# Cross-attention with a gated residual on one core: the last stage reordered, and its residual added by VectorE from a loaded x

## The chip, the cores and the metric

The kernel runs on one core of a Trainium2 chip. The metric is the device time of one execution in microseconds, lower is better. TensorE (PE), VectorE (DVE), ScalarE (ACT), GpSimd (POOL) and SyncE (SP) run their own instruction streams and wait for each other through semaphores; SP issues most of the transfers.

## The reference

x is (4, 1024, 1024), ctx (4, 2048, 512), all float32.

```python
memory_proj = jnp.einsum('bme,de->bmd', memory, W_mem)
scores = jnp.einsum('bnd,bmd->bnm', hidden_states, memory_proj) / jnp.sqrt(jnp.float32(D))
attn = jax.nn.softmax(scores, axis=-1)
memory_context = jnp.einsum('bnm,bmd->bnd', attn, memory_proj)
gate_input = jnp.concatenate([hidden_states, memory_context], axis=-1)
gate = jax.nn.sigmoid(jnp.einsum('bnf,df->bnd', gate_input, W_gate) + b_gate)
fused = hidden_states + gate * memory_context
return _rmsnorm(fused, norm_w)      # fused * rsqrt(mean(fused^2) + 1e-6) * norm_w
```

## The kernel before

The 4096 rows of x are 32 units of 128 rows; two units are a pair, 16 pairs (NPAIR). Each operand of a matmul is split into a rounded part and a remainder (ACT rounds, DVE subtracts), and a product runs three passes.

Four stages follow each other. The first makes q (x times W_mem) and weights for the gate. The second computes, pair by pair, the part of the gate that comes from x ("zx", with the bias), in seven products of 12 matmuls, and stores it. The third is the attention: scores, softmax, exchange of the probabilities through DRAM, and the weighted sum of memory, am, stored for each unit. The **last stage**, about 1270 us to the end, is the one that changes. For each pair it multiplies am (256 rows, 512 columns) by two weight matrices of 512 x 1024: one gives the other part of the gate, one the memory context. Each is done in Strassen's manner with seven products of half size ("gate 1" to "gate 7", "context 1" to "context 7"; `gate_product` and `context_product` on PE), six matmuls of 512 columns each, so a pair is 14 products, 84 matmuls. The tile of a pair has two units u and two halves h of 512 columns; a quadrant is (u, h).

What belongs to a pair p in the last stage:

- DVE: `gate_part` (line 1264) adds a product in PSUM to the loaded zx in place, six times (products 2 to 7). `transpose_am` (line 253), `sums_of_am` (line 1222) and `split_at` (line 305) prepare the operands of the next pair. `context_part` (line 1270) adds a product to a copied one in the output tile `c_u`, twice. `gated` (line 1278) multiplies a context quadrant by its gate into `c_u`, four times; (1, 0) is done at the start of the next pair. `scale` (line 1284) multiplies a unit of `c_u` by the norm factor and the norm weights.
- ACT: `seed_z` (line 856), `gate` (the sigmoid, line 861), `copy_c` (three copies of a product, line 865), `split_at` (line 792), `square` (line 871) with the sum over a row.
- POOL: `add_xres` (line 648), two transfers that add x to `c_u` in SBUF, each after the last gated products of its unit; `inverse_root` (lines 653, 656), the norm factor.
- SP: `load_zx` (line 586), `load_am` (line 582), `store_out` (line 592), in that order in `pair_out`.

Gate tile and `c_u` are double buffered by the parity of the pair. The orders are written out by hand in each engine's program. In a pair's stretch DVE and ACT also square and scale the pair before: `square(p - 1)` and `scale(p - 1)`. PE's first product of a pair waits until all of DVE's six gate parts of the pair before are done (`gz_ev`), and context 1 until its last `gated` is done (`gc_ev`):

```python
def pair_c(p, par, first=False):
    gate_product(p, par, 1)
    context_product(p - 1, 1 - par, 7, first=first)
    gate_product(p, par, 2)
    gate_product(p, par, 3)
    for n in range(1, 5):
        context_product(p, par, n)
        gate_product(p, par, n + 3)
    context_product(p, par, 5)
    context_product(p, par, 6)
```

For the last pair the kernel before already loads x into `c_xlast` and adds it on DVE (`residual`, line 1474).

Of the kernel before, what the change touches and what calls it, by code (L numbers as in the profile page):

```python
# [5 lines left out]
ALU = mybir.AluOpType  # L6
# [14 lines left out]
def build(nc, x, mem, w_mem, w_gate, b_gate, norm_w, out):  # L21
# [28 lines left out]
    with ExitStack() as ctx:  # L50
# [121 lines left out]
        c_xlast = F[:, 28 * KW:36 * KW]  # L172
# [48 lines left out]
        nw_loaded, xlast_loaded = sem("nw_loaded"), sem("xlast_loaded")  # L221
# [4 lines left out]
        xres_added = [sem(f"xres_added{u}") for u in range(2)]  # L226
        fused_done, sq_done, var_done, rstd_done = sem("fused_done"), sem("sq_done"), sem("var_done"), sem("rstd_done")
        out_ready, out_stored = sem("out_ready"), [sem(f"out_stored{r}") for r in range(2)]
# [98 lines left out]
        COPY_B, COPY_22, COPY_12 = range(1, 4)  # L327
# [6 lines left out]
        def _(sp):  # L334
# [255 lines left out]
            def store_out(p, par, u):  # L590
                sp.wait_ge(out_ready, p * 2 + (u + 1))
                sp.dma_start(out_rows[bass.ds(p * (2 * P) + u * P, P), :], unit_tile(c_u[par], u)
                             ).then_inc(out_stored[par], 16)
# [8 lines left out]
            for n in range(NPROD):  # L602
# [7 lines left out]
            sp.dma_start(c_xlast.rearrange("p (u d) -> p u d", u=2),  # L610
                         x_rows[ROWS - 2 * P:ROWS, :].rearrange("(u p) d -> p u d", u=2)).then_inc(xlast_loaded, 16)
# [14 lines left out]
            pair_out(1, 1)  # L626
# [4 lines left out]
            pair_out(NPAIR - 1, 1, ahead=False, am_ahead=False)  # L631
            store_out(NPAIR - 1, 1, 0)
            for n, h in enumerate((1, 0)):
                sp.wait_ge(out_ready, NUNIT + n)
                sp.dma_start(out_rows[ROWS - P:ROWS, BANK * h:BANK * (h + 1)], quad(c_u[1], 1, h)
                             ).then_inc(out_stored[1], 16)
            sp.wait_ge(out_stored[0], 16 * NPAIR)
            sp.wait_ge(out_stored[1], 16 * (NPAIR + 1))

        @block.gpsimd  # L640
        def _(pool):
# [17 lines left out]
            def pair_pool(p, par):  # L659
                for u in range(2):  # L660
                    add_xres(p, par, u)
# [11 lines left out]
        def _(act):  # L673
# [193 lines left out]
            def square(p, par, u, wait=True):  # L867
                act.wait_ge(xres_added[u], p * 16 + 16)
# [6 lines left out]
            def pair_act(p, par, i=None, norm=True, following=True):  # L875
# [3 lines left out]
                if i is not None:  # L879
# [841 lines left out]
```

## Time and profile before

| | us |
|---|---|
| median of 3 runs (lowest, highest) | 1581.92 (1580.89, 1583.91) |
| the profiled execution | 1583.89 |
| its span | 1582.2 |
| PE busy | 1536.3 (97%) |
| DVE busy | 1046.1 (66%) |
| ACT busy | 541.0 (34%) |
| POOL busy | 53.8 (3%) |

The span is from the first to the last instruction of one profiled execution. The PE row counts matmuls, whose records overlap by some 0.16 us. Times in the rows below are microseconds from the start of the span.

### The profile page before, as it was taken

To read this page: it belongs to the slowest core of one execution; us is meant where nothing else is said; L and a number is where in the kernel's file an instruction comes from. 1 tells how busy PE (TensorE), PEld (TensorE's weight loads), DVE (VectorE), ACT (ScalarE), POOL (GpSimd) and SP (SyncE) were. 2 spreads that over 40 slices of the span, in tenths; PEclk is the share of its full clock that TensorE was granted. 3 is DMA by queue.
4 is the path that set the end of the run, shared out by engine and by line. 5 is a ranking of instruction groups with operands and counts; after the bars stand their busy time and mean duration, and the time that the engine had idled before them with its cause. 6 is when DMAs were issued, how large, how long until landed. Compare 5 with 4: busy or idle time off the path is not lost.

```text
span 1582.2 us, 21437 instructions
## 1 busy us (share of the span) xinstructions
PE 1536.3 (97%) x6720; PEld 1262.2 (80%) x6720; DVE 1046.1 (66%) x1474; ACT 541.0 (34%) x915; POOL 53.8 (3%) x100
## 2 busy tenths in 40 slices
PE   6999999999999989999999999999999999999996
PEld 5888888888888768888888878888788877777775
DVE  5654758777778754477437754476555877777776
ACT  4233342222222332243222522244222644444443
POOL 0000000000000000000000000000000011111112
PEclk9999999999999999999999999999999999999998
DMA  9998436333332766747584658656766676666663
GB/s 194 234 236 186 117 98 170 112 107 106 106 106 93 200 152 183 179 140 183 156 209 132 172 140 196 169 152 167 180 211 207 233 202 182 184 181 182 183 183 116
DMA packets 213637, 262.59 MB, mean 166 GB/s; under 512 B 19552, under 2 KB 136288, under 8 KB 213344
## 3 DMA queue, kind: packets, MB, share of 16 engines
q1 hardware_dynamic: 209280, 246.48, 57.3%
q0 software_dynamic: 4320, 15.73, 5.1%
q14 instruction: 27, 0.22, 0.1%
q8 instruction: 10, 0.16, 0.0%
HBM read 170.39 MB, written 89.65 MB: 164 GB/s over the span
## 4 chain that ended last, share of the span: by engine, by line
PE 28%; DMA 16%; issue 7%; DVE 7%; ACT 3%; SPq 2%; DVEq 0%; ACTq 0%; POOLq 0%; POOL 0%
PE bank L1506 26%; DMA region_f<-in_x 8%; DMA prob_scratch<-prob 4%; DMA region_f<-in_ctx 2%; PE bank L1638 2%; DMA region_f<-prob_scratch 1%; DVE region_f L1278 1%; DVE region_l L305 1%; DVE region_f L1270 1%; SPq L246 1%; DMA am_out<-q_scratch 1%; DVE max_part L1182 1%; SPq L447 1%; DVE region_n L305 1%; ACT prob L778 0%
## 5 line engine op out<-in xcount | busy, mean ns | idle before, releaser
L1506 PE MATMUL bank<-region_t,region_l 128*128 128x512 f32 x1536 | 355.9, 391 | 5.9 <-DVE region_l L305 3.7
L1506 PE MATMUL bank<-region_n,region_l 128*128 128x512 f32 x1536 | 355.9, 391 | 5.4 <-DVE region_n L305 3.8
L1506 PEld LDWEIGHTS bank<-region_t,region_l 128*128 128x128 f32 x1536 | 288.8, 188 | 68.9 <-issue 9.0
L1506 PEld LDWEIGHTS bank<-region_n,region_l 128*128 128x128 f32 x1536 | 288.9, 188 | 67.5 <-issue 5.5
L1506 PE MATMUL bank<-region_t,region_n 128*128 128x512 f32 x960 | 219.7, 391 | 12.5 <-DVE region_t L305 12.5
L1506 PEld LDWEIGHTS bank<-region_t,region_n 128*128 128x128 f32 x960 | 181.1, 189 | 50.7 <-DVE region_t L305 13.0
L806 ACT CAST region_l<-bank 128x512 fp32r<-128x512 f32 x128 | 75.0, 586 | 346.3 <-DVE bank L1211 346.1
L1211 DVE STREAM_TRANSPOSE bank<-region_f 128x512 f32<-128x512 f32 x128 | 88.8, 716 | 122.8 <-DMA region_f<-prob_scratch 120.6
L305 DVE TENSOR_TENSOR region_t<-region_f,region_t 128x1024 fp32r<-128x1024 f32 (+2 forms) x77 | 110.6, 1468 | 75.9 <-ACT region_t L682 60.0
L1547 PE MATMUL bank<-region_t,region_l 128*128 128x512 f32 x576 | 135.8, 389 | 0.0
L1638 PE MATMUL bank<-region_t,region_l 128*128 128x512 f32 x480 | 122.3, 393 | 10.6 <-DVE region_f L1264 5.3
L1547 PEld LDWEIGHTS bank<-region_t,region_l 128*128 128x128 f32 x576 | 108.1, 188 | 22.5
L1638 PE MATMUL bank<-region_n,region_l 128*128 128x512 f32 x480 | 120.5, 389 | 0.0
L1638 PEld LDWEIGHTS bank<-region_t,region_l 128*128 128x128 f32 x480 | 88.9, 188 | 34.6 <-issue 16.8
L778 ACT ACTIVATE prob<-bank,neg_max 128x512 f32<-128x512 f32 x128 | 86.2, 686 | 76.9 <-DVE neg_max L1188 73.7
L1638 PEld LDWEIGHTS bank<-region_n,region_l 128*128 128x128 f32 x480 | 90.1, 188 | 18.9
L733 ACT CAST region_l<-region_f 128x512 fp32r<-128x512 f32 x80 | 49.5, 623 | 158.7 <-PE bank L1547 146.5
L305 DVE TENSOR_TENSOR region_l<-bank,region_l 128x512 fp32r<-128x512 f32 x128 | 86.6, 676 | 10.5 <-ACT region_l L806 10.4
L1547 PE MATMUL bank<-region_n,region_l 128*128 128x512 f32 x384 | 92.2, 389 | 0.0
L1182 DVE TENSOR_REDUCE max_part<-bank 128x1 f32<-128x512 f32 x128 | 84.4, 660 | 10.5 <-PE bank L1506 10.5
L305 DVE TENSOR_TENSOR region_n<-region_f,region_n 128x512 fp32r<-128x512 f32 (+3 forms) x70 | 78.7, 1141 | 15.8 <-ACT region_n L678 7.8
L305 DVE TENSOR_TENSOR region_l<-region_f,region_l 128x512 fp32r<-128x512 f32 (+2 forms) x120 | 81.9, 686 | 10.0 <-ACT region_l L792 9.4
(81 smaller groups left out, 1401.9 us busy)
## 6 DMA issues: line engine op xcount, KB each, us to landing
region_f<-in_ctx SPq DMA_DIRECT2D x128, 256.0 KB, 5.5
prob_scratch<-prob SPq DMA_DIRECT2D x128, 256.0 KB, 2.7
region_f<-prob_scratch SPq DMA_DIRECT2D x128, 256.0 KB, 4.4
region_f<-in_x SPq DMA_DIRECT2D x64, 256.0 KB, 6.1
region_f<-in_x SPq DMA_DIRECT2D x128, 128.0 KB, 2.7
out<-region_f SPq DMA_DIRECT2D x31, 512.0 KB, 2.6
region_f<-in_x POOLq DMA_DIRECT2D x30, 512.0 KB, 8.9
q_scratch<-prob SPq DMA_DIRECT2D x8, 1024.0 KB, 6.4
```

Source lines behind the costliest of these rows:

```text
L246: eng.dma_start(v[SQ * q:SQ * (q + 1), :, lo:hi], src[:, chunk * q + lo:chunk * q + hi].rearrange("(b i) f -> i b f", i=SQ)).then_inc(sign ...
L305: return nc.vector.tensor_tensor(dst, src, hi.bitcast(F32), ALU.subtract)
L447: sp.dma_start(v[SQ * q:SQ * (q + 1)], mem[b, r:r + P, :].rearrange("(s i) c -> i s c", i=SQ)).then_inc(mn_loaded[j], 16)
L733: nc.scalar.copy(z_x[i][:, HI], quarter(z_f[i])).then_inc(z_hi, 1)
L778: nc.scalar.activation(prob[:, BANK * j:BANK * (j + 1)], bank[j][:], ACT.Exp, bias=neg_max[:], scale=SCALE, accum_out=sum_part[:, j:j + 1] ...
L806: nc.scalar.copy(b_pt[:, HI, TPB * g:TPB * (g + 1), :].rearrange("p k n -> p (k n)"), ps_t[g % 2][:]).then_inc(pt_hi, 1)
L1182: nc.vector.reduce_max(max_part[:, j:j + 1], bank[j][:], AX_X).then_inc(max_done, 1)
L1211: nc.vector.transpose(ps_t[g % 2][:].rearrange("p (k b i) -> p k b i", k=TPB, i=SQ), v[:, TPB * g:TPB * (g + 1)]).then_inc(pt_t, 1)
L1270: nc.vector.tensor_tensor(v, ps[:], v, ALU.add).then_inc(gc_ev, 1)
L1506: mm = nc.tensor.matmul(dst, lhs(a), rhs(b), start=first and n == 0, stop=last and n == len(PASSES) - 1)
L1547: mm = nc.tensor.matmul(ps[:], z_x[i][:, a, t, :], z_w[i][:, b, t, :], start=opens and t == 0 and n == 0, stop=closes and t == HT - 1 and ...
L1638: mm = nc.tensor.matmul(ps[:], x[:, a, P * t:P * (t + 1)], w[n][:, b, t, :], start=opens and t == 0 and m == 0, stop=closes and t == CH - ...
```

## The change

The last stage gets another order and another way to add x. `c_xlast` becomes `c_xres`: SP loads both units of x for each pair into it (`load_xres`), when the addition of the pair before is done, and DVE adds a whole unit of it to `c_u` (`residual_unit`) behind the unit's last gated quadrant; POOL's accumulating transfers go. In DVE's `pair_c` the scalings are those of pair p - 2 and stand behind gate parts 2 and 3; gate part 7 stands directly behind `gated(0, 0)`. In ACT's `pair_act` the squares of pair p - 1 go to the end of the pair, and the copy for (0, 1) before the one for (1, 1), each with a wait for its own unit's store. SP's `pair_out` stores pair p - 2 behind the two loads, and before the load of am. The last pair has its own order, with the additions by quadrant.

```diff
@@ sync
+            def load_xres(p):
+                sp.dma_start(c_xres.rearrange("p (u d) -> p u d", u=2),
+                             x_rows[bass.ds(p * (2 * P), 2 * P), :].rearrange("(u p) d -> p u d", u=2)
+                             ).then_inc(xres_loaded, 16)
...
-            def pair_out(p, par, ahead=True, am_ahead=True):
+            def pair_out(p, par, ahead=True, stored=True, am_ahead=True):
                 if ahead:
                     sp.wait_ge(gc_ev, p * NGEV)
                     load_zx(p + 1, 1 - par)
+                sp.wait_ge(fused_done, p * 2)
+                load_xres(p)
+                if stored:
+                    for u in range(2):
+                        store_out(p - 2, par, u)
                 if am_ahead:
                     sp.wait_ge(ca_t, p * 2 + 4)
                     load_am(p + 2)
-                for u in range(2):
-                    store_out(p - 1, 1 - par, u)
@@ gpsimd
-            def add_xres(p, par, u):
-                pool.wait_ge(gc_ev, p * NGEV + (U12, U21)[u])
-                pool.dma_start(unit_tile(c_u[par], u), x_rows[bass.ds(p * (2 * P) + u * P, P), :], accum_op=ALU.add
-                               ).then_inc(xres_added[u], 16)
@@ scalar
             def square(p, par, u, wait=True):
-                act.wait_ge(xres_added[u], p * 16 + 16)
+                act.wait_ge(fused_done, p * 2 + (u + 1))
...
-            def pair_act(p, par, i=None, norm=True, following=True):
+            def pair_act(p, par, i=None, following=True):
                 seed_z(p)
                 copy_c(p, 1, cb[:], ca)
                 gate(p, par, 0, 0, Z11)
-                if i is not None:
-                    act.wait_ge(out_stored[par], i * 32)
-                copy_c(p, 2, quad(c_u[par], 1, 1), cf)
                 if following:
                     act.wait_ge(gc_prod, p * NPROD)
                     act.wait_ge(ca_t, p * 2 + 4)
                     split_at(1 - par, at_12, atf_12)
-                if norm:
-                    square(p - 1, 1 - par, 0, wait=i is not None)
                 gate(p, par, 1, 1, Z22)
+                if i is not None:
+                    act.wait_ge(out_stored[par][0], i * 16)
                 copy_c(p, 3, quad(c_u[par], 0, 1), ca)
                 if following:
                     act.wait_ge(ca_sum, p * 4 + 8)
                     split_at(1 - par, at_s, atf_s)
+                if i is not None:
+                    act.wait_ge(out_stored[par][1], i * 16)
+                copy_c(p, 2, quad(c_u[par], 1, 1), cf)
+                if following:
+                    gate(p, par, 0, 1, Z12)
                     split_at(1 - par, at_22, atf_22)
-                if norm:
-                    square(p - 1, 1 - par, 1)
-                gate(p, par, 0, 1, Z12)
-                gate(p, par, 1, 0, Z21)
+                square(p - 1, 1 - par, 0, wait=i is not None)
+                if following:
+                    gate(p, par, 1, 0, Z21)
+                square(p - 1, 1 - par, 1)
+                if not following:
+                    gate(p, par, 0, 1, Z12)
+                    gate(p, par, 1, 0, Z21)
@@ vector
+            def residual_unit(p, par, u):
+                dve.wait_ge(xres_loaded, p * 16 + 16)
+                dve.wait_ge(gc_ev, p * NGEV + (U12, U21)[u])
+                v = unit_tile(c_u[par], u)
+                nc.vector.tensor_tensor(v, v, unit_tile(c_xres, u), ALU.add).then_inc(fused_done, 1)
+
-            def pair_c(p, par, i=None, norm=True, following=True):
+            def pair_c(p, par, i=None, following=True):
                 gated(p - 1, 1 - par, 1, 0, ca[:], product=7)
+                residual_unit(p - 1, 1 - par, 1)
                 dve.wait_ge(zx_loaded[par], (1 if i is None else i + 1) * 16)
                 gate_part(p, par, 2, zf, 1, 1)
+                if i is not None:
+                    scale(p - 2, par, 0)
                 gate_part(p, par, 3, za, 0, 1)
+                if i is not None:
+                    scale(p - 2, par, 1)
+                gate_part(p, par, 4, zb, 0, 0)
                 if following:
                     transpose_am(p + 1, c_ain_units)
-                gate_part(p, par, 4, zb, 0, 0)
+                gate_part(p, par, 5, za, 1, 1, Z22_OPEN)
                 if following:
                     sums_of_am(p + 1)
-                gate_part(p, par, 5, za, 1, 1, Z22_OPEN)
-                if following:
                     split_at(p + 1, 1, 1 - par, at_12, atf_12)
                 gate_part(p, par, 6, zf, 0, 1, Z12_OPEN)
                 if following:
                     split_at(p + 1, 2, 1 - par, at_s, atf_s)
                 if i is not None:
-                    dve.wait_ge(out_stored[par], i * 32)
+                    dve.wait_ge(out_stored[par][0], i * 16)
+                if not following:
+                    scale(p - 1, 1 - par, 0)
                 gated(p, par, 0, 0, cb[:], product=4)
+                gate_part(p, par, 7, za, 1, 0)
                 if following:
                     split_at(p + 1, 3, 1 - par, at_22, atf_22)
-                if norm:
-                    scale(p - 1, 1 - par, 0)
-                gate_part(p, par, 7, za, 1, 0)
                 context_part(p, par, 5, COPY_22, ca, 1, 1)
-                if norm:
+                if not following:
                     scale(p - 1, 1 - par, 1)
-                context_part(p, par, 6, COPY_12, cf, 0, 1)
-                gated(p, par, 1, 1, quad(c_u[par], 1, 1), opened=U22_OPEN)
-                gated(p, par, 0, 1, quad(c_u[par], 0, 1), opened=U12_OPEN)
+                if following:
+                    context_part(p, par, 6, COPY_12, cf, 0, 1)
+                    gated(p, par, 1, 1, quad(c_u[par], 1, 1), opened=U22_OPEN)
+                    gated(p, par, 0, 1, quad(c_u[par], 0, 1), opened=U12_OPEN)
+                    residual_unit(p, par, 0)
...
-            dve.wait_ge(xlast_loaded, 16)
-            residual(1, (1,), U22)
-            residual(0, (0, 1), U12)
+            dve.wait_ge(xres_loaded, 16 * NPAIR)
+            residual(0, 0, U11)
+            context_part(LP, 1, 6, COPY_12, cf, 0, 1)
+            gated(LP, 1, 1, 1, quad(c_u[1], 1, 1), opened=U22_OPEN)
+            gated(LP, 1, 0, 1, quad(c_u[1], 0, 1), opened=U12_OPEN)
+            residual(1, 1, U22)
+            residual(0, 1, U12)
             gated(LP, 1, 1, 0, ca[:], product=7)
-            residual(1, (0,), U21)
+            residual(1, 0, U21)
```

## Rows read from the trace of the kernel before

**Rows 1.** The page: busy time, share of the span and instructions of each engine.

```profile
PE 1536.3 (97%) x6720; PEld 1262.2 (80%) x6720; DVE 1046.1 (66%) x1474; ACT 541.0 (34%) x915; POOL 53.8 (3%) x100
```

**Rows 2.** Stretches: length, busy time by engine, clock, DMA share; second stage, then last.

```profile
318.69:337.73 19.04, 19.04 (x85) 15.77 (x84) 14.55 (x21) 4.36 (x7) 0.00 (x0) 1.00 0.33 110
...
1330.00:1350.07 20.07, 19.32 (x85) 15.70 (x85) 14.94 (x24) 8.60 (x16) 3.29 (x6) 1.00 0.65 183
```

**Rows 3.** Timeline of PE: start, length, instruction, count, idle before it.

```profile
1269.06 1.62 PE L1638 MATMUL bank<-region_t,region_l 128*128 128x512 f32 x6 [0.23 <-DVE region_l L305]
...
1346.51 2.88 PE L1638 MATMUL bank<-region_n,region_t 128*128 128x512 f32 x12
1350.07 1.65 PE L1638 MATMUL bank<-region_t,region_l 128*128 128x512 f32 x6 [0.67 <-DVE prob L1264]
...
1352.93 2.88 PE L1638 MATMUL bank<-region_t,region_l 128*128 128x512 f32 x12
...
1550.06 1.65 PE L1638 MATMUL bank<-region_t,region_l 128*128 128x512 f32 x6 [0.43 <-DVE prob L1264]
```

**Rows 4.** Timeline of DVE at the start of pair 1, then around a later turn.

```profile
1272.71 0.69 DVE L1278 TENSOR_TENSOR region_f<-bank,prob 128x512 f32<-128x512 f32 x1
...
1345.96 1.23 DVE L305 TENSOR_TENSOR region_l<-region_f,region_l 128x1024 fp32r<-128x1024 f32 x1 [1.19 <-ACT region_l L792]
1347.10 0.68 DVE L1278 TENSOR_TENSOR region_f<-bank,prob 128x512 f32<-128x512 f32 x1
1347.70 0.43 DVE L305 TENSOR_TENSOR region_l<-region_f,region_l 128x256 fp32r<-128x256 f32 x1
1348.06 1.27 DVE L1284 SCALAR_TENSOR_TENSOR region_f<-region_f,rstd 128x1024 f32<-128x1024 f32 x1
1349.26 0.68 DVE L1264 TENSOR_TENSOR prob<-bank,prob 128x512 f32<-128x512 f32 x1
...
1352.25 1.28 DVE L1278 TENSOR_TENSOR region_f<-region_f,prob 128x512 f32<-128x512 f32 x2
...
1355.85 0.69 DVE L1264 TENSOR_TENSOR region_f<-bank,region_f 128x512 f32<-128x512 f32 x1 [0.67 <-PE bank L1638]
```

**Rows 5.** The chain that ended last: start, length, what.

```profile
1334.17 8.56 DMA region_f<-in_x
```

**Rows 6.** Groups on DVE with their shapes, last stage: busy time, mean ns.

```profile
L305 DVE TENSOR_TENSOR region_l<-region_f,region_l 128x256 fp32r<-128x256 f32 x15 | 6.4, 424 | 0.0
...
L1474 DVE TENSOR_TENSOR region_f<-region_f 128x1024 f32<-128x1024 f32 x1 | 1.2, 1219 | 0.0
```

**Rows 7.** DMA issues of the last stage: size, median us to landing.

```profile
out<-region_f SPq DMA_DIRECT2D x31, 512.0 KB, 2.6
...
prob<-zx_scratch SPq DMA_DIRECT2D x7, 1024.0 KB, 5.9
```

**Rows 8.** Stretches of 1 us, as rows 2; the last two columns are DMA share, GB/s.

```profile
1246.00:1247.00 1.00, 1.00 (x6) 0.82 (x5) 0.97 (x3) 0.59 (x1) 0.00 (x0) 1.00 0.95 324
...
1251.00:1252.00 1.00, 1.00 (x6) 0.84 (x5) 0.95 (x2) 0.79 (x2) 0.00 (x0) 1.00 1.08 434
...
1359.00:1360.00 1.00, 1.00 (x6) 0.80 (x6) 1.00 (x4) 0.70 (x2) 0.00 (x0) 1.00 1.11 205
```

**Rows 9.** Timeline of POOL.

```profile
1347.67 0.55 POOL L656 TENSOR_TENSOR rstd<-mean_sq,minus_half 128x1 f32<-128x1 f32 x1
...
1561.94 0.56 POOL L656 TENSOR_TENSOR rstd<-mean_sq,minus_half 128x1 f32<-128x1 f32 x1
```

**Rows 10.** Timelines of ACT (first row) and DVE behind pair 15's start.

```profile
1560.44 1.06 ACT L871 ACTIVATE region_n<-region_f 128x1024 fp32r<-128x1024 f32 x1
...
1565.40 0.69 DVE L1278 TENSOR_TENSOR region_f<-bank,region_f 128x512 f32<-128x512 f32 x1 [0.72 <-ACT region_f L861]
...
1573.40 0.68 DVE L1278 TENSOR_TENSOR region_f<-bank,region_f 128x512 f32<-128x512 f32 x1
1574.12 0.69 DVE L1474 TENSOR_TENSOR region_f<-region_f 128x512 f32<-128x512 f32 x1
```

More of the change, by code:

```diff
@@ L171, in build @@
         c_ain = f_block[7]
-        c_xlast = F[:, 28 * KW:36 * KW]
+        c_xres = F[:, 28 * KW:36 * KW]
         c_square = R2[:, 56 * KW:60 * KW]
@@ L225, in build @@
         gc_prod, gc_copy, gc_ev = sem("gc_prod"), sem("gc_copy"), sem("gc_ev")
-        xres_added = [sem(f"xres_added{u}") for u in range(2)]
         fused_done, sq_done, var_done, rstd_done = sem("fused_done"), sem("sq_done"), sem("var_done"), sem("rstd_done")
-        out_ready, out_stored = sem("out_ready"), [sem(f"out_stored{r}") for r in range(2)]
+        out_ready = sem("out_ready")
+        out_stored = [[sem(f"out_stored{r}{u}") for u in range(2)] for r in range(2)]
         HALVES = ("G1a", "G1b", "X0a", "X0b", "E0a", "X1a", "X1b", "E0b", "X2a", "X2b", "E1a", "X3a", "X3b", "E1b",
@@ L326, in build @@
         U11, U22_OPEN, U12_OPEN, U22, U12, U21 = range(1, 7)
-        COPY_B, COPY_22, COPY_12 = range(1, 4)
+        COPY_B, COPY_12, COPY_22 = range(1, 4)
         GATE = {(0, 0): 1, (1, 1): 2, (0, 1): 3, (1, 0): 4}
@@ L631, in _ @@
             pair_out(NPAIR - 1, 1, ahead=False, am_ahead=False)
+            for u in range(2):
+                store_out(NPAIR - 2, 0, u)
             store_out(NPAIR - 1, 1, 0)
@@ L635, in _ @@
                 sp.dma_start(out_rows[ROWS - P:ROWS, BANK * h:BANK * (h + 1)], quad(c_u[1], 1, h)
-                             ).then_inc(out_stored[1], 16)
-            sp.wait_ge(out_stored[0], 16 * NPAIR)
-            sp.wait_ge(out_stored[1], 16 * (NPAIR + 1))
+                             ).then_inc(out_stored[1][1], 16)
+            for u in range(2):
+                sp.wait_ge(out_stored[0][u], 16 * (NPAIR // 2))
+                sp.wait_ge(out_stored[1][u], 16 * (NPAIR // 2 + u))
         @block.gpsimd
@@ L659, in pair_pool @@
             def pair_pool(p, par):
-                for u in range(2):
-                    add_xres(p, par, u)
                 for u in range(2):
@@ L908, in _ @@
             gate(0, 0, 1, 1, Z22)
+            copy_c(0, 3, quad(c_u[0], 0, 1), ca)
             copy_c(0, 2, quad(c_u[0], 1, 1), cf)
-            copy_c(0, 3, quad(c_u[0], 0, 1), ca)
             act.wait_ge(ca_t, 4)
@@ L1460, in _ @@
             gated(0, 0, 0, 1, quad(c_u[0], 0, 1), opened=U12_OPEN)
+            residual_unit(0, 0, 0)
             dve.wait_ge(nw_loaded, 16)
@@ L1465, in _, with residual @@
                     pair_c(i * 2 + par, par, i)
-            pair_c(NPAIR - 2, 0, NPAIR // 2 - 1)
             LP = NPAIR - 1
+            pair_c(LP - 1, 0, NPAIR // 2 - 1)
             pair_c(LP, 1, NPAIR // 2 - 1, following=False)
-            def residual(u, hs, count):
-                cols = slice(D * u + BANK * hs[0], D * u + BANK * (hs[-1] + 1))
+            def residual(u, h, count):
+                v = quad(c_u[1], u, h)
                 dve.wait_ge(gc_ev, LP * NGEV + count)
-                nc.vector.tensor_tensor(c_u[1][:, cols], c_u[1][:, cols], c_xlast[:, cols], ALU.add
-                                        ).then_inc(fused_done, 1)
+                nc.vector.tensor_tensor(v, v, quad(c_xres, u, h), ALU.add).then_inc(fused_done, 1)
             def last_square(h, count):
                 v = quad(c_u[1], 1, h)
-                dve.wait_ge(fused_done, count)
+                dve.wait_ge(fused_done, 2 * LP + count)
                 nc.vector.tensor_tensor_reduce(out=quad(c_gate[0], 1, h), in0=v, in1=v, scale=1.0 / D, scalar=0.0,
```

18 lines of the change are left out of this document (8 added, 10 removed).

## Prediction

> **What bounds the kernel now.** I read the page's engine shares first: TensorE (PE) is busy for 97% of the span, VectorE (DVE) for 66% [rows 1]. So a gain in the last stage can only be time in which PE stands still there. The busy time of each engine, pair by pair, says how much that is [rows 2]. In the stage that computes the input half of the gate, a pair of units also takes 84 matmuls of the same shape, and PE does them in 19.04 us with no idle time, 1.36 us for each product of six, in a hardware loop that turns every pair. In the last stage the same 84 matmuls take 20.07 us, at the same granted clock (1.00). PE's timeline shows where the difference sits [rows 3]: the two products that began at 1346.51 should have given way at 1349.23 (2 x 1.36 later), but the next pair's first starts at 1350.07, a gap of 0.84 us; and the first two of that pair take 2.86 us (to 1352.93) instead of 2.72. The first gate product of pair 1 starts at 1269.06 and that of pair 15 at 1550.06, so 14 pairs take 281.00 us (20.07 each) where 14 x 19.04 = 266.56 would do. **14.44 us is all that the stage's steady part can give.**
>
> Why does PE wait? DVE's timeline [rows 4]: the gate's last part (line 1264, product 7 of the pair) runs at 1349.26, and the next pair's first product needs the bank that it frees; PE starts 0.12 us after it ends. Product 7 itself was done at 1346.51, so that part is 2.6 us late. In front of it DVE waited 1.19 us for ScalarE's (ACT's) rounding of the sums, and then did the subtraction (1345.96), the gated product (1347.10), the last subtraction and a scaling (1348.06, 1.27 us). The chain that ended last goes on [rows 5]: ACT's rounding stands behind the square of the pair before, and that waits for the accumulating transfer of x, 8.56 us from 1334.17, which starts when the last gated product is done. So each pair hangs on the one before through a transfer, at a period of 20.07 us.
>
> **The change, step by step.** I count time T from the start of a pair's first product. PE's order is gate 1, context 7 of the pair before, gate 2, gate 3, context 1, gate 4, context 2, gate 5, context 3, gate 6, context 4, gate 7, context 5, context 6; the k-th ends at 1.36k. DVE or ACT takes a product up 0.20 us after its end (the two from 1352.93 end at 1355.65, the part for the second runs at 1355.85 [rows 3, 4]); I take 0.3 where it waits for two things. A DVE operation of 512 columns takes the engine for 0.60 us (two from 1352.25 are through in 1.28, the last 0.08 of which overlap), a scaling for 1.20 us (1348.06 to 1349.26) [rows 4].
>
> *Removed:* both accumulating transfers and ACT's wait for them. *Added on DVE:* two additions of 1024 columns for each pair. The one of this form in the trace took 1219 ns [rows 6]; a subtraction of the same size takes 1.23 us, and the engine is taken for 1.14 us (1345.96 to 1347.10) [rows 4], and 0.12 us more where the operation in front is the one it reads (1573.40 to 1574.12 instead of 0.60) [rows 10]. That is 2.5 us for each pair. DVE is busy 14.94 us of a pair now [rows 2] and would be at 17.4 of 19.04.
>
> *Moved on DVE:* the part for gate 7 goes directly behind the gated product (0,0), both scalings (now of the pair two back) to early in the pair, the additions to the end (unit 0) and the start (unit 1). Laid out: the gated product (1,0) of the pair before at T 3.3 to 3.9, addition 4.0 to 5.1, part 2 to 5.7, scaling to 6.9, part 3 to 7.5, scaling to 8.7, part 4 to 9.3, transposes to 10.5, part 5 at 11.2 (the product ends at 10.88), sums to 13.3, subtraction to 13.9, part 6 to 14.5, subtraction of the sums 14.5 to 15.7, gated product (0,0) to 16.3, **part 7 at 16.5 to 17.2**, last subtraction to 17.5, context 5 at 17.9, context 6 at 19.3, two gated products to 21.1, addition to 22.3. That last is T 3.3 of the next pair, so the layout closes on a period of 19.04. PE needs part 7 by 19.04 (1.8 us to spare), the gated product (1,0) by 5.44, where context 1 starts (1.4 us), part 3 by 9.52, part 5 by 14.96. I cost the two additions at nothing because of these covers; if the second cover went, every further microsecond on DVE would be one on PE.
>
> *Moved on ACT:* its row of work is 8.6 us of a pair [rows 2]. The roundings no longer stand behind a square that waits: sums at about T 13.4 to 14.4. The two copies into the output tile now come at T 12.4 and 14.4 and wait for the stores of the pair two back.
>
> *Moved on SP:* the load of zx goes out at T 4.1, then a new load of x (1 MB), two stores at T 7.2 and 9.0 behind scalings that are now early, then the load of am. The stores are issued behind two loads of 1 MB. A store alone lands in 2.6 us and a load of zx in 5.9 [rows 7]. How long the store waits is not shown, so I bound it. Bytes: loads issued back to back moved 324 to 434 GB/s (seven of 512 KB from wm: the slowest and the fastest whole microsecond of 1246 to 1257); while the accumulating transfers run, it is 205 at full share [rows 8]. With about 400 GB/s, two loads and a store (2.62 MB) are through 6.6 us after the first packet at T 5.0, so the first copy's store lands at about T 11.9, before T 12.4. If the transfers were strictly one after another at their landing times, 4.1 + 5.9 + 5.9 + 2.6 = T 18.5. ACT's copy has 2.4 us to spare before it would push part 7 past 19.04 (rounding 1.0, subtraction 1.14, gated product 0.6, part 7 0.7 behind it), so T 14.8 decides, which needs 276 GB/s. I take the bytes, for the slowest row of queued plain loads lies above that rate [rows 8].
>
> The Trainium skill, "DMA: Bandwidth & Descriptors", section on queues, rings and completion order, says that descriptors of one issuing engine's row are consumed in ring order. By it the stores, which today find an empty queue, would stand behind both loads, as in the layout; it doesn't change the rate. It is why I give this a rival of its own.
>
> GpSimd (POOL) keeps two tiny operations for each unit, 0.2 and 0.56 us [rows 9], at other times. One of them ran from 1347.67 to 1348.22 with DVE's subtraction of 256 columns at 1347.70 inside it; that took 0.43 us, the mean of all 15 is 424 ns [rows 4, 6, 9], and the scaling at 1348.06 took the usual 1.27 us. So I charge nothing. The Trainium skill, "SBUF — State Buffer", section "SBUF: two separate sides", says that a DVE operation with two SBUF inputs and a GpSimd one that reads SBUF exclude each other. By it the two extra additions could lose up to 2 x 0.56 us for each pair, leaving 0.3 us of the 1.4 us cover; these rows show no such loss.
>
> *Start.* Pair 1's context 1 starts 5.56 us behind 1269.06 (four products, the first two at 2.86), at 1274.62. It waits for DVE's gated product (1,0) of pair 0, which ran at 1272.71 [rows 4]. Before that DVE must now do the addition of unit 0, so the gated product runs from 1273.97 to 1274.65, and PE starts 0.12 us after it and loses another 0.14: 0.3 us lost. *End.* Behind pair 15 the work is on DVE [rows 10]: gated product (0,0) at T 15.34, an unbroken row to the last addition at T 24.1. In the new order the row begins with the scaling of (14, 0), at T 15.6, where ACT and POOL have the factor (square from T 13.5, factor 2.1 us behind its start as at 1560.44 to 1562.50 [rows 9, 10]), and holds the same operations: 0.2 us later. The pair's end is otherwise the same.
>
> Sum: 14.44 - 0.3 - 0.2 = 13.9 us. The profiled execution took 1583.89 us (span 1582.2), and 1570.0 would be left; that execution lies 1.97 us above the median of 1581.92, so **1568.0 us** at the median.
>
> **The rivals.** *DVE takes PE's place in part (chance 0.17).* For: 17.4 us of 19.04 is little idle time, the order is fixed, and DVE already waits 1 to 2 us in places for PE's products, which can't all be used. Against: the layout leaves 1.4 us at the tightest point, and the input stage runs PE without a gap with DVE busy 14.56 of 19.04 [rows 2] (no row shows 17). It decides when the gated product (1,0) ends behind T 5.3. If DVE's round came to 19.4 us, 0.36 x 14 = 5 us would be lost and the time be about 1573; it reaches "no change" at a round of 20.0.
>
> *The stores come late (chance 0.06, the other side).* ACT's copy into the tile waits for the store of the pair two back, which stands behind 2 MB of loads. By landing times in a row, T 18.5 against 14.8: 3.7 us in each of 14 pairs, a period of 22.7 where it is 20.07 now: 1581.9 + 14 x 2.6 = 1619. At 250 GB/s the store lands at T 15.8, 1.0 us late, and the gain is gone. For: the queue's order. Against: rows 8.
>
> *The gap isn't the gate part (chance 0.04).* If PE paid the 0.9 us for something else at a pair's turn, nothing but the start and the end would move: 1581 to 1583. Against: the input stage has such a turn for each pair and pays nothing [rows 2].
>
> *As laid out:* 0.73.
>
> **How the numbers follow.** A change of 0.2% (3.2 us) is about what a measurement of this kernel can tell from none. The forecast, 1568.0, has its own range of 1566.5 to 1570 (14.44 us and a little at the end at best; a start or end dearer by 2 us at worst). With the part of the first rival in which DVE's round stays below 19.5 the range is 1566.3 to 1575. Faster: 0.73, nearly all of the first rival and a little of the second: 0.89. The same: the last rival and the edge of the others, 0.05. Slower: 0.06.
>
> **What would show it.** Right: first gate products 19.04 us apart, from about 1269 to 1536; "DVE L1264" gone from what PE waits for; no transfer of x in the chain; DVE busy about 17.3 us for each pair; the POOL queue's traffic gone, SP's 16 MB more; stores landing later than 2.6 us after their issue, but ACT not waiting for them. Wrong: PE waiting for line 1278 before context 1 (the first rival), ACT waiting for DMA before line 865 (the second), a period of 20 us with part 7 at T 16.5 (the third).

## The result and the profile after

The changed kernel takes 1571.8 us at the median of 4 runs (1571.13 to 1575.41), beside 1582.91 before: a ratio of 0.9932 (95% interval 0.9919 to 0.9944). That is 11.1 us less; 13.9 were forecast, and the time lies inside the range. The profiled execution is the slowest of the four: 1575.41 us, span 1573.6. So its own gain is 8.6 us of span, and the rows below show somewhat more waiting than the other three executions can have had.

The page of the kernel after: engine shares, then DMA issues (median us to landing), which answer to [rows 1, 7].

```profile
PE 1536.4 (98%) x6720; PEld 1263.1 (80%) x6720; DVE 1078.2 (69%) x1505; ACT 541.9 (34%) x915; POOL 36.4 (2%) x70
...
region_f<-in_x SPq DMA_DIRECT2D x16, 1024.0 KB, 8.1
out<-region_f SPq DMA_DIRECT2D x31, 512.0 KB, 7.1
```

PE does the same work; DVE has 32 us more. The stores land 7.1 us behind their issue instead of 2.6 [rows 7]. Stretches from one first gate product to the next answer to [rows 2]:

```profile
1308.13:1327.67 19.54, 19.33 (x86) 15.70 (x85) 16.99 (x26) 8.60 (x16) 2.24 (x5) 1.00 0.52 189
1347.43:1367.01 19.58, 19.32 (x84) 15.70 (x85) 16.98 (x26) 8.59 (x16) 2.23 (x5) 1.00 0.52 187
1406.12:1425.32 19.20, 19.20 (x86) 15.59 (x84) 16.56 (x25) 8.17 (x16) 1.90 (x4) 1.00 0.54 191
```

From one first gate product to the next a pair takes 19.1 to 19.9 us where it took 20.07 [rows 2], and 19.04 is what PE needs. PE's timeline, as in [rows 3]:

```profile
1269.58 1.63 PE L1662 MATMUL bank<-region_t,region_l 128*128 128x512 f32 x6 [0.23 <-DVE region_l L305]
...
1327.67 1.65 PE L1662 MATMUL bank<-region_t,region_l 128*128 128x512 f32 x6 [0.21 <-DVE region_f L1272]
...
1347.43 1.65 PE L1662 MATMUL bank<-region_t,region_l 128*128 128x512 f32 x6 [0.36 <-DVE prob L1272]
...
1541.22 1.52 PE L1662 MATMUL bank<-region_t,region_l 128*128 128x512 f32 x6
```

Fourteen pairs take 1541.22 - 1269.58 = 271.64 us instead of 281.00, so 9.36 us are gained there; 266.56 would be free of gaps, so 5.1 us are left, 0.3 of them at pair 1. Behind pair 15's start come 32.38 us where there were 32.14 (a loss of 0.24), and the stage starts 0.52 us later, for reasons in front of it: 9.36 - 0.24 - 0.52 = 8.6.

What still holds PE is again gate part 7 (now line 1272). Why it is late stands in the waits of the last stage (engine, line, waited for: us in total, times, longest), and in the chain around pair 2's end:

```profile
ACT region_f L869 <- DMA out<-region_f: 28.4, 11, 3.1
...
DVE region_l L305 <- ACT region_l L796: 15.2, 7, 2.7
DVE region_t L305 <- ACT region_t L796: 12.2, 6, 2.3
```

```profile
1294.87 1.28 DVE region_f L1292
1296.32 7.59 DMA out<-region_f
1304.06 0.43 issue
1304.49 1.06 ACT region_l L796
...
1307.31 0.68 DVE prob L1272
```

No transfer of x is in the chain, as forecast. In its place stands a store. Pair 2 began at 1289.06, so the store of the scaling goes out at T 7.3 and lands at T 14.9 (the prediction had 11.9), ACT's copy and the rounding of the sums wait for it, and part 7 runs at T 18.25 instead of 16.5. It ends at T 18.9, just in time here (19.07 us to the next pair's start) and up to 0.9 us late in other pairs.

### The profile page after: what moved, and what is told of

It is laid out like the page before. It is cut to its first block, busy times and chain, and to the rows that moved or that the text cites. A ratio compares the mean times of both kernels' runs of the same rounds, so it can differ in the third digit from the quotient of the medians.

```text
span 1573.6 us, 21461 instructions
## 1 busy us (share of the span) xinstructions
PE 1536.4 (98%) x6720; PEld 1263.1 (80%) x6720; DVE 1078.2 (69%) x1505; ACT 541.9 (34%) x915; POOL 36.4 (2%) x70
## 4 chain that ended last, share of the span: by engine, by line
PE 33%; DMA 13%; DVE 6%; issue 5%; SPq 3%; ACT 2%; DVEq 0%; ACTq 0%; POOL 0%; POOLq 0%
PE bank L1530 23%; PE bank L1662 10%; DMA prob_scratch<-prob 5%; DMA out<-region_f 3%; DMA region_f<-in_ctx 2%; SPq L246 2%; DMA region_f<-prob_scratch 2%; DMA am_out<-q_scratch 1%; DVE region_l L305 1%; DVE region_f L1286 1%; DVE max_part L1190 1%; DVE region_f L1292 1%; SPq L447 1%; ACT prob L782 1%; DVE region_n L305 0%
## 5 line engine op out<-in xcount | busy, mean ns | idle before, releaser
L305 DVE TENSOR_TENSOR region_l<-region_f,region_l 128x512 fp32r<-128x512 f32 (+2 forms) x120 | 81.8, 686 | 17.8 <-ACT region_l L796 17.1
```

The source lines that it names most:

```text
L305: return nc.vector.tensor_tensor(dst, src, hi.bitcast(F32), ALU.subtract)
```

## The experiments

All ratios are to the kernel before, from runs of five rounds or more. T is counted as in the prediction. The pace of each is taken from its trace: first gate product of pair 1 to that of pair 15, 14 pairs; the last three context products start 16.32 us (12 x 1.36) behind the latter. The pace is used because the start of the stage alone lies between 1268.1 and 1272.7 in the thirteen profiled executions, though the stages in front of it are as before; medians that differ by 1 or 2 us tell little.

**1. The load of x reads a scratch tensor.** My first theory of the late store was that x itself is slow to read: 217 to 258 GB/s flow while it runs.

```diff
             def load_xres(p):
-                             x_rows[bass.ds(p * (2 * P), 2 * P), :].rearrange("(u p) d -> p u d", u=2)
+                             zx_dram[bass.ds(p * (2 * P), 2 * P), :].rearrange("(u p) d -> p u d", u=2)
```

> The changed kernel, but the 1 MB load that feeds VectorE's addition reads the zx scratch tensor instead of x (so the residual added is zx, not x). Theory A (the load of x is slow because of where it reads: 217 to 258 GB/s at full DMA share while it runs, against some 400 for the scratch tensors; the stores behind it land at T 14.9 instead of 11.9, ScalarE's copy waits up to 3.1 us and gate part 7 comes late): the load lands in about 5 us instead of 8.1, the stores in about 4 to 5 instead of 7.2, first products of the pairs are 19.04 us apart, and the ratio to the kernel before is 0.990 to 0.9915 (the changed kernel had 0.9932). Rival B (VectorE is too full with the two additions and is late by itself): nothing moves, 0.993, and the same five or six gaps before gate product 1.

Measured: 1571.99 us, 0.9932 (0.9919 to 0.9946). The load landed in 8.0 us instead of 8.1, the stores in 7.0, and ACT still waited 22.0 us for them. So the source is not the reason. The full DVE (rival B) was not excluded by this run (it had forecast 0.993 here).

**2. The stores ahead of the load of x.**

```diff
-                sp.wait_ge(fused_done, p * 2)
-                load_xres(p)
                 if stored:
                     for u in range(2):
                         store_out(p - 2, par, u)
+                sp.wait_ge(fused_done, p * 2)
+                load_xres(p)
```

> The changed kernel with SP's load of x behind the two stores instead of ahead of them. Theory A: the stores stand behind the load of zx alone and land about 3 to 4 us after their issue, at T 10 to 11, ahead of ScalarE's copy at T 12.4; x lands at about T 18, before the addition at T 21; no gaps on TensorE; ratio 0.990 to 0.9915. Rival B: 0.993. If x came too late after all, VectorE would wait for a transfer before the addition, and it would be slower than the changed kernel.

Measured: 1570.22 us, 0.9921 (0.9906 to 0.9936), a little above the forecast 0.990 to 0.9915, into which the interval reaches. One stretch of its trace, DVE around gate part 7 in that pair (it began at 1326.73), the DMA issues, and PE's start of the last three products:

```profile
1326.73:1345.77 19.04, 19.04 (x86) 15.77 (x84) 17.16 (x25) 8.60 (x15) 1.77 (x5) 1.00 0.54 193
```

```profile
1342.36 0.68 DVE L1286 TENSOR_TENSOR region_f<-bank,prob 128x512 f32<-128x512 f32 x1
1343.25 0.69 DVE L1272 TENSOR_TENSOR prob<-bank,prob 128x512 f32<-128x512 f32 x1 [0.21 <-PE bank L1662]
...
1349.12 0.68 DVE L1286 TENSOR_TENSOR region_f<-bank,prob 128x512 f32<-128x512 f32 x1
```

```profile
out<-region_f SPq DMA_DIRECT2D x27, 512.0 KB, 3.0
region_f<-in_x SPq DMA_DIRECT2D x13, 1024.0 KB, 5.7
```

```profile
1269.21 1.62 PE L1662 MATMUL bank<-region_t,region_l 128*128 128x512 f32 x6 [0.23 <-DVE region_l L305]
...
1552.49 4.24 PE L1662 MATMUL bank<-region_n,region_l 128*128 128x512 f32 x18
```

This is the prediction's layout: PE busy for 19.04 of 19.04 us, DVE for 17.16, part 7 at T 16.52, the gated product (1,0) at T 3.35 of the next pair. 1552.49 - 16.32 - 1269.21 = 266.96 us: no gap but the 0.4 us at pair 1. What the profiled execution of the changed kernel had above that (4.7 of its 5.1 us) hung on the place of two instructions in SP's queue. Rival B, a DVE too full by itself, is out: DVE has the same work here.

**3. The order alone.** x is still added by accumulating transfers; nothing is added on DVE but in the last pair. (Of the diff against the changed kernel, the main lines.)

```diff
-                sp.wait_ge(fused_done, p * 2)
-                load_xres(p)
...
             def pair_pool(p, par):
+                for u in range(2):
+                    add_xres(p, par, u)
...
             def square(p, par, u, wait=True):
-                act.wait_ge(fused_done, p * 2 + (u + 1))
+                act.wait_ge(xres_added[u], p * 16 + 16)
...
-                residual_unit(p - 1, 1 - par, 1)
...
-                    residual_unit(p, par, 0)
```

> The new order of the last stage alone, with x still added by POOL's accumulating transfers (no additions on VectorE but in the last pair). Theory A: the squares come at T 16 of the next pair, where the transfers (8.9 us behind T 21 and T 4 of the next) have landed by T 13, so nothing waits for them; the stores share the engines with them and land at about T 11 to 14; period 19.04 to 19.2, ratio 0.990 to 0.992. So the order would be what gives the time, and the additions on VectorE cost up to 3 us. Rival B expects the same here, for VectorE is 2.4 us emptier. Rival C (the gain comes from the additions, which take the transfer out of the chain): 0.998 to 1.0.

Measured: 1583.13 us, 1.0000 (0.9991 to 1.0009). This is a miss of mine: nothing in front of gate part 7 waits for the transfers of x, and yet nothing is gained. The ratio is the one of rival C, but not for rival C's reason, as experiment 6 shows. The chain of one pair (it began at 1387.44) and the wait:

```profile
1392.47 1.29 DVE region_f L1298
...
1393.93 9.30 DMA out<-region_f
...
1403.81 1.06 ACT region_t L802
...
1406.63 0.69 DVE region_f L1278
```

```profile
ACT region_f L875 <- DMA out<-region_f: 42.5, 13, 3.5
```

The store went out at T 6.5 behind the load of zx, beside the transfers of x, and landed 9.3 us later, at T 15.8; part 7 ran at T 19.2 and the pair took 20.01 us. A wait for a store had taken the place of the wait for the transfer.

**4. The additions alone**, in the old order; POOL's transfers go, and the square waits for the addition.

```diff
@@ sync, pair_out of the kernel before
                     load_zx(p + 1, 1 - par)
+                sp.wait_ge(fused_done, p * 2)
+                load_xres(p)
@@ vector, pair_c of the kernel before
                 gated(p - 1, 1 - par, 1, 0, ca[:], product=7)
+                residual_unit(p - 1, 1 - par, 1)
...
                 gated(p, par, 0, 1, quad(c_u[par], 0, 1), opened=U12_OPEN)
+                if following:
+                    residual_unit(p, par, 0)
```

> The old order of the last stage with x loaded for each pair and added by VectorE. The layout by hand: ScalarE's square of unit 0 no longer waits, rounding of the sums at T 13.4, subtraction to T 15.7, gated product to 16.3, last subtraction, scaling to 17.8, gate part 7 to T 18.5, in time for 19.04 with 0.4 us to spare; the stores go out at T 18 and 20 into an empty queue. Then the ratio is 0.990 to 0.992 here too, and either half of the change would do alone. If the order is needed (rival C turned round, or rival B), gate part 7 behind the scaling is late by 0.2 to 0.6 us in each pair: 0.993 to 0.997.

Measured: 1569.81 us, 0.9921 (0.9908 to 0.9935). Part 7 (line 1263 there) still stands behind a scaling, but the square in front of the roundings no longer waits. The pair began at 1326.54:

```profile
1326.54:1345.58 19.04, 19.04 (x85) 15.77 (x84) 16.89 (x27) 8.47 (x16) 2.01 (x4) 1.00 0.51 190
```

```profile
1343.11 1.28 DVE L1283 SCALAR_TENSOR_TENSOR region_f<-region_f,rstd 128x1024 f32<-128x1024 f32 x1
1344.30 0.68 DVE L1263 TENSOR_TENSOR prob<-bank,prob 128x512 f32<-128x512 f32 x1
```

Part 7 at T 17.8 to 18.4 is in time. So the additions alone give all of it, and the order gives nothing on top. If anything it costs 1 or 2 us (0.9932 beside 0.9921, intervals that overlap), for it puts the stores behind two loads; here they are issued at T 18.0 and at T 1.4 of the next pair and land in 2.6 us.

**5. The two places that wait moved.** The kernel before, transfers kept.

```diff
@@ scalar, pair_act of the kernel before
-                if norm:
-                    square(p - 1, 1 - par, 0, wait=i is not None)
                 gate(p, par, 1, 1, Z22)
...
                     split_at(1 - par, at_22, atf_22)
                 if norm:
+                    square(p - 1, 1 - par, 0, wait=i is not None)
                     square(p - 1, 1 - par, 1)
@@ vector, pair_c of the kernel before
-                if norm:
-                    scale(p - 1, 1 - par, 0)
                 gate_part(p, par, 7, za, 1, 0)
                 context_part(p, par, 5, COPY_22, ca, 1, 1)
                 if norm:
+                    scale(p - 1, 1 - par, 0)
                     scale(p - 1, 1 - par, 1)
```

> The kernel before, with x still added by POOL's accumulating transfers, and only the places that wait for them moved: ScalarE's square of unit 0 behind its roundings (it stood ahead of them), and VectorE's first scaling behind gate part 7 and context part 5. Theory D (what the change removes is only the wait for the transfer ahead of the roundings; the accumulating transfer itself costs nothing): roundings at T 13.4, part 7 at T 16.6 to 17.3, square of unit 0 at T 14.8 behind a transfer that lands at T 12.4, period 19.04, ratio 0.991 to 0.993, as with the additions alone (0.9921). Rival: the accumulating transfers slow something else (the stores or the loads of zx and am, as in the run of the order alone), and the ratio is 0.996 to 1.0.

Measured: 1571.91 us beside 1583.9, 0.9924 (0.9910 to 0.9937), 14 pairs in 266.68 us. The transfers still take 8.6 us for unit 0 and 11.3 us for unit 1, and cost the pace nothing where nothing in front of gate part 7 waits for them. This run moves two things, the square that waits and a scaling of 1.2 us. Experiment 4, where the scaling stays, shows that taking the wait away is enough. Whether moving the scaling alone would be enough was not tested: by [rows 4], part 7 directly behind the last subtraction would start at 1348.06 (T 18.1) and end at T 18.7, ahead of 19.04 even with the wait in place (an estimate). Behind pair 15's start this run spends 33.22 us, the changed kernel 32.38 and 32.25 (run 9), so its time is no better than the changed kernel's although its pace is.

**6. The order alone, stores ahead of the load of zx.**

```diff
@@ to experiment 3
+                if stored:
+                    for u in range(2):
+                        store_out(p - 2, par, u)
                 if ahead:
                     sp.wait_ge(gc_ev, p * NGEV)
                     load_zx(p + 1, 1 - par)
-                if stored:
-                    for u in range(2):
-                        store_out(p - 2, par, u)
```

> The new order alone with accumulating transfers, as in the run of that name (ratio 1.0, stores landing 9.1 us after their issue, ScalarE waiting 42.5 us for them in 13 pairs), but SP issues the two stores ahead of the load of zx. Theory: the gain of the order alone is lost to stores that stand behind the load of zx and share the DMA engines with the accumulating transfers; ahead of it they land in 4 to 7 us, before T 13.5, and the ratio is 0.991 to 0.994; zx lands by about T 19, in time for T 23. Rival: the accumulating transfers alone keep the stores until T 15 or later, whatever the queue's order: 0.996 to 1.0.

Measured: 1569.54 us, 0.9911 (0.9898 to 0.9925), 14 pairs in 266.68 us, stores landing in 5.7 us. Against experiment 3, 13.6 us between the medians for the place of two instructions. The rival, that the transfers of x alone would keep the stores, is out.

**7, 8 and 11. How much DVE can still take.** Extra additions of 512 columns into an unused tile, ahead of the addition of unit 0, in pairs 2 to 14 (13 pairs; the expectations count 14): two of them on experiment 2 (run 7) and on experiment 4 (run 8), four on experiment 2 (run 11).

```diff
+            def pad(p):
+                for k in range(2):        # 4 in run 11
+                    if k:
+                        dve.wait_ge(pad_done, (p - 2) * 2 + k)
+                    nc.vector.tensor_tensor(am_out[:], c_nw[:, 0:BANK], c_nw[:, BANK:2 * BANK], ALU.add
+                                            ).then_inc(pad_done, 1)
...
+                    if i is not None:
+                        pad(p)
                     residual_unit(p, par, 0)
```

> The changed kernel with the stores ahead of the load of x (0.9921), and two more VectorE additions of 512 columns into an unused tile, 1.3 us in all, ahead of the addition of unit 0, in 14 pairs. VectorE's layout has 1.4 us to spare before context product 1 and gate part 7 keeps its 1.7 us: no gap on TensorE or one of 0.1 us for each pair, ratio 0.992 to 0.993. If the cover is smaller than the layout says, up to 1.3 us x 14 = 18 us are added: up to 1.004.

> The same two extra additions, 1.3 us, in the kernel with the old order and the additions of x on VectorE (0.9921). There the gated product (1,0) ends at T 4.85 in its trace, 0.5 us ahead of what context product 1 needs, so 0.7 us and 0.14 us of refilling are lost in each of 14 pairs: 10 to 12 us, ratio 0.999 to 1.0. If the order gives no cover of its own, it stays at 0.992 to 0.993 as in the new order.

> The changed kernel with the stores ahead of the load of x and four extra VectorE additions of 512 columns in 14 pairs, 2.6 us in all (two cost nothing). The layout has 1.4 us to spare at the gated product (1,0), and VectorE's work is then 17.4 + 2.6 = 20.0 us for each pair. So 1.2 to 1.4 us are lost in each pair, 14 x 1.3 = 18 us more than with two: ratio 1.002 to 1.005. It says where VectorE becomes the bound, the first rival of the prediction.

Measured: run 7 1570.17 us, 0.9922 (0.9908 to 0.9935), pairs of 19.04 to 19.06 us. Run 8 1580.82 us, 0.9978 (0.9969 to 0.9987), which is less than the 0.999 to 1.0 forecast. Run 11 1589.43 us, 1.0035 (1.0023 to 1.0048), as forecast. PE's timeline of run 8, then of run 11:

```profile
1335.61 1.65 PE L1656 MATMUL bank<-region_n,region_l 128*128 128x512 f32 x6 [0.51 <-DVE region_f L1277]
...
1355.45 1.65 PE L1656 MATMUL bank<-region_n,region_l 128*128 128x512 f32 x6 [0.51 <-DVE region_f L1277]
```

```profile
1335.50 1.66 PE L1671 MATMUL bank<-region_n,region_l 128*128 128x512 f32 x6 [1.06 <-DVE region_f L1286]
...
1355.98 1.67 PE L1671 MATMUL bank<-region_n,region_l 128*128 128x512 f32 x6 [1.15 <-DVE region_f L1286]
```

Both wait at context product 1 for the gated product (1,0), the point that the prediction's first rival names. In the old order 1.3 us of DVE work costs 0.8 us a pair (19.84); in the new order 1.3 us cost nothing and 2.6 us cost 1.4 (20.48 and 20.4 in turn). Some 0.14 us of each loss is PE's restart (two products in 2.86 us instead of 2.72 [rows 3]), so about 0.6 us were free in the old order and 1.3 us in the new one. The new order has some 0.7 us more room on DVE. That is what it is worth, and this kernel has no use for it.

**9 and 10. The changed kernel again, and the stores ahead of both loads.**

```diff
@@ run 10, to experiment 2
+                if stored:
+                    for u in range(2):
+                        store_out(p - 2, par, u)
                 if ahead:
                     sp.wait_ge(gc_ev, p * NGEV)
                     load_zx(p + 1, 1 - par)
-                if stored:
-                    for u in range(2):
-                        store_out(p - 2, par, u)
```

> The changed kernel itself once more, beside the two below and the same runs of the kernel before. Its first products had periods of 19.2 to 19.9 us where its stores came late. It should be at 0.9925 to 0.994, 1 to 3 us above the one with the stores ahead of both loads.

> The changed kernel with SP's two stores ahead of the load of zx too, so that they find an empty queue. They land in 2.6 to 3 us, at T 9.5 to 12; zx goes out at about T 9.2 and x behind it at T 10.4, which lands at about T 18, ahead of the addition at T 21. Period 19.04 as with the stores ahead of x alone: 0.990 to 0.992. If x comes later than T 21.1, VectorE waits for it and the time rises.

Measured: the changed kernel 1571.82 us, 0.9931 (0.9917 to 0.9945); its profile has span 1570.0 and 14 pairs in 268.71 us, so 2.2 us over the pace and not 5.1. Run 10: 1570.85 us, 0.9921 (0.9907 to 0.9935), stores in 2.7 us, x in 7.7, 14 pairs in 266.96. It is as fast as experiment 2. The intervals of the two kernels overlap; that the stores cost the changed kernel 1 to 2 us is not shown by the times alone. It is read from the pace in the traces (268.71 and 271.64 us beside 266.96), and the medians of experiments 2, 4 and 10 all lie below the changed kernel's.

## Why the prediction came out as it did

*The number and the range.* The measured 1571.8 us lies inside 1566.3 to 1575, but above the 1566.5 to 1570 that the prediction gave to the forecast itself. The rest of the range was there for a DVE that takes PE's place, which did not happen; that the loss from the stores fell into it was luck. The kernel before, run beside it, took 1582.91 us instead of 1581.92, so 13.9 us of gain would have been 1569.0.

*What bounds the kernel.* Right. The 14.44 us at gate part 7 were all there was: the pace of 19.04 us was reached in experiments 2, 4, 5, 6, 7 and 10, and none went below it. Experiments 4 and 5 show the cause together: the gap is gone when the wait is taken away with the scaling left in place, and it is gone with the transfers kept and the places that wait for them moved.

*DVE's additions at nothing.* Right. They take 1225 ns each (1219 forecast), DVE is busy 17.16 us of a pair (17.4), and the layout's times hold within 0.1 us. That POOL's small operations would cost DVE nothing was taken from one overlap, 0.43 us beside a mean of 424 ns over the same fifteen operations, which is thin; it came out right (416 ns on average in the changed kernel). The rival with a chance of 0.17, DVE in PE's place, decides where it was said to, at context product 1, and only with more than some 1.3 us of extra work (runs 7 and 11; 1.4 forecast).

*The moves on SP.* This is the step that failed: "two loads and a store (2.62 MB) are through 6.6 us after the first packet at T 5.0, so the first copy's store lands at about T 11.9". It landed at T 14.9 in pair 2, and between T 14.5 and 15.7 in pairs 2 to 14. The threshold beside it, T 14.8, was about right (0.03 us lost in pair 2, 0.9 in pair 6, where the store landed at T 15.7), so the rival with a chance of 0.06 came in part: not 3.7 us for each pair but 0 to 0.9. Two of the signs of being right failed with it: part 7 was still what PE waits for, and ACT waited for stores. I had taken 400 GB/s from a stretch in full flow. The stretches of 1 us after pair 2's loads (the last two columns are DMA share and GB/s):

```profile
1294.00:1295.00 1.00, 1.00 (x6) 0.81 (x6) 1.00 (x3) 0.00 (x0) 0.00 (x0) 1.00 0.68 86
1295.00:1296.00 1.00, 1.00 (x6) 0.84 (x5) 1.00 (x1) 0.00 (x0) 0.00 (x0) 1.00 0.80 324
1296.00:1297.00 1.00, 1.00 (x7) 0.81 (x6) 1.00 (x3) 0.57 (x1) 0.00 (x0) 1.00 1.02 422
1297.00:1298.00 1.00, 1.00 (x6) 0.84 (x5) 1.00 (x2) 0.00 (x0) 0.00 (x0) 1.00 0.92 336
1298.00:1299.00 1.00, 1.00 (x6) 0.84 (x5) 1.00 (x2) 0.43 (x1) 0.00 (x0) 1.00 0.79 217
1299.00:1300.00 1.00, 1.00 (x6) 0.81 (x6) 0.75 (x2) 0.42 (x2) 0.00 (x0) 1.00 0.94 246
1300.00:1301.00 1.00, 1.00 (x6) 0.84 (x5) 0.76 (x2) 0.44 (x2) 0.00 (x0) 1.00 0.89 258
1301.00:1302.00 1.00, 1.00 (x7) 0.81 (x6) 0.96 (x4) 0.60 (x1) 0.00 (x0) 1.00 1.01 414
1302.00:1303.00 1.00, 1.00 (x6) 0.84 (x5) 1.00 (x3) 0.00 (x0) 0.00 (x0) 1.00 1.03 422
1303.00:1304.00 1.00, 1.00 (x6) 0.83 (x5) 0.64 (x1) 0.00 (x0) 0.00 (x0) 1.00 1.03 418
```

These ten stretches end at 1304.00, the first store landed at 1303.91, and together they moved 3.14 MB in 9.9 us, 317 GB/s. So two things were wrong in the sum. It counted two loads and one store, 2.62 MB, but most of the second store, and a little of the load of am behind it, had moved too before the first store had landed: 0.5 MB more, 1.3 us at 400 GB/s. And the rate was 317 instead of 400: 2.0 us for 3.14 MB. 317 GB/s is even above the 276 that the prediction had called enough; with the bytes that really moved, it wasn't. Why the second store's bytes move ahead of the first one's landing was not looked into.

The rate is lost in two places. The first microsecond flows at 86 GB/s, and three of the later ones at 217 to 258. The slow start is there in experiments 2 and 4 too (37 and 49 GB/s). The second stretch is shorter or absent there. In experiment 4, with the same two loads of 1 MB and no store behind them, x lands in 7.1 us instead of 8.1. In experiment 2, with the stores ahead of x, x flows at 324 to 381 GB/s in the pair that began at 1326.73, but in the other pairs from 2 to 14 one microsecond goes at 180 to 246, with the stretches cut from the pair's start (209 in 1318.69 to 1319.69). So a slow microsecond also comes without stores behind the load, and why it lasts three of them in the changed kernel was not settled. It isn't the tensor that is read (experiment 1).

The Trainium skill, "DMA: Bandwidth & Descriptors", section on queues, rings and completion order, says that on each DMA engine the descriptors of one issuing engine's row are consumed in ring order. These runs agree: a store lands in 2.7 us when no load was issued just ahead of it (run 10), in 3.0 behind zx issued some 3 us earlier (2), and in 7.2 behind both loads.

*Removing the transfers.* I cut the change into "removed" and "moved" and gave the gain to both together. The experiments part them: the additions alone 0.9921, the order alone 1.0000 (0.9911 with its stores ahead of the load of zx), both 0.9932. So either half is enough by itself, if the stores are not late. On top of the additions, the order's only effect on the time was the one on the stores.

*Start and end.* 0.3 us and 0.2 us forecast, 0.3 and 0.24 measured.

*The sum.* 14.44 - 0.3 - 0.2 became, in the profiled execution, 14.44 - 5.1 - 0.24 (and 0.52 from in front of the stage), and about 11.1 at the median. The mis-sized term is the store's landing, 3 us late: 0.5 MB too few in its bytes and 400 GB/s where 317 flowed.

## What to carry to other kernels

Lay the stage out on one clock, with each hand-over, before judging a reordering: it showed that the whole gap hangs on one late operation, and the gap went whichever way that chain was shortened (here by additions on another engine, or by moving one square and one scaling). When an output buffer's store is issued earlier, look at what now stands ahead of it in its queue: moving two store instructions ahead of one load was worth 13.6 us in one kernel here and some 1.6 us in the changed one (runs 9 and 2, a difference inside their intervals). And a transfer of 1 MB should not be timed at the rate of full flow; the first whole microsecond of these carried a quarter of it or less. When a landing is added up from bytes, count what is issued right behind the transfer too: here most of it had moved by then.

## What the runs showed of the hardware

- With two stores queued behind it, a load of 1 MB flows at 217 to 258 GB/s for some 3 us (the changed kernel); with the stores ahead, it is one microsecond at 180 to 246 in twelve of thirteen pairs, and 295 at the lowest in the other (experiment 2, stretches of 1 us cut from the pair's start).
- Two stores of 512 KB stood behind two loads of 1 MB in one queue. When the first store landed, 3.14 MB had moved, where the two loads and that store are 2.62 MB (the changed kernel, pair 2).
- POOL's two tiny operations became longer, not DVE's: they take 0.39 and 0.89 us in the rows below (unit 1; unit 0's take 0.40 and 0.55), where they took 0.19 and 0.55 before (0.55 in [rows 9]). DVE's new additions aren't the only reason: in experiment 3, which has none, the two average 378 and 710 ns, and in experiment 4, which has them in the old order, 441 and 550. The order matters too. A POOL timeline of the changed kernel:

```profile
1309.78 0.39 POOL L659 TENSOR_TENSOR mean_sq<-sq_mean,norm_eps 128x1 f32<-128x1 f32 x1 [0.78 <-ACT region_n L875]
1310.25 0.89 POOL L662 TENSOR_TENSOR rstd<-mean_sq,minus_half 128x1 f32<-128x1 f32 x1
```

DVE's two gated products ran from 1309.44 and its addition from 1310.76, each at its usual length. The Trainium skill, "SBUF — State Buffer", section "SBUF: two separate sides", says that such a DVE operation and a GpSimd one that reads SBUF exclude each other. The trace agrees in part: POOL's operations are longer beside the gated products, but the second one ended at 1311.14, inside the addition, which was not longer (1225 ns on average over all 30). What decides isn't settled: with DVE's subtraction of 256 columns starting 0.02 or 0.03 us later, the second operation took 0.84 us in experiment 2 (at 1343.84) and 0.55 in the kernel before (1347.67). DVE lost nothing that the pace shows.
